# Thirty-eight dummy products on TensorE behind tile 0's scores in a gated cross-attention kernel

## What is computed

```python
x = x + tanh(g_xattn) * xattn(layernorm(x), ctx)
x = x + tanh(g_ffn) * ffn(layernorm(x))
# xattn, 16 heads of 32; with 128 context rows only the image branch has keys
q = rms_norm(xn @ q_w.T + q_b) * norm_q
k = rms_norm(ctx @ k_img_w.T + k_img_b) * norm_k_img
v = ctx @ v_img_w.T + v_img_b
out = softmax(q k^T / sqrt(32)) v  per head, then @ o_w.T + o_b
# ffn, hidden 2048, both weights made ternary in groups of 64
h = relu(xn @ ternary(W_fc).T) ** 2
y = rms_norm(h) @ ternary(W_proj).T
```

## Time and profile before

| | us |
|---|---|
| median of 3 runs | 923.18 |
| the runs | 922.71, 923.18, 924.92 |
| the profiled execution's own time | 922.2 |
| its span (first to last instruction) | 920.4 |
| TensorE busy in the span | 873.2 |
| ScalarE busy | 801.4 |
| VectorE busy | 709.5 |
| mean granted clock of TensorE | 0.985 |

### The profile page before, as it was taken

One profiled execution on the slowest core, in us unless ns is written; L12 is line 12 of the kernel. 1 busy time (PEld: TensorE's weight loads), 2 busy tenths in 40 slices (PEclk: granted clock), 3 DMA queues, 4 the chain that ended last, 5 costly groups with the idle time before them and its releaser, 6 DMA issues.

```text
span 920.4 us, 22304 instructions
## 1 busy us (share of the span) xinstructions
PE 873.2 (95%) x7493; PEld 526.6 (57%) x7589; DVE 709.5 (77%) x1546; ACT 801.4 (87%) x1608; POOL 559.8 (61%) x616
## 2 busy tenths in 40 slices
PE   6687789999999999999999999999999999999998
PEld 3243455556556666555566665556566655666675
DVE  6989999988788787878788787878878787876301
ACT  5988999898998888899998888998988889889674
POOL 2312346777667666667677666666776666756476
PEclk9887999999999999999999999999999999999999
DMA  8849676577657766666577656676767556764401
GB/s 346 213 105 206 139 164 110 104 140 128 126 117 127 136 113 101 123 127 128 118 132 126 120 102 122 122 131 116 134 126 123 120 105 124 129 102 84 81 13 47
DMA packets 319890, 115.78 MB, mean 126 GB/s; under 512 B 305184, under 2 KB 305440, under 8 KB 318240
## 3 DMA queue, kind: packets, MB, share of 16 engines
q1 hardware_dynamic: 319776, 114.34, 63.3%
HBM read 30.67 MB, written 8.39 MB: 42 GB/s over the span
## 4 chain that ended last, share of the span: by engine, by line
PE 79%; ACT 3%; issue 2%; POOL 1%; DVE 1%; POOLq 0%; ACTq 0%; DVEq 0%
PE mix_pair L594 12%; PE up_pair L578 11%; PE up_pair L579 11%; PE mix_pair L593 9%; PE score_pair L533 5%; PE score_pair L532 5%; PE score_pair L531 5%; PE mix_pair L531 3%; PE score_ps L533 3%; PE mix_pair L532 3%; PE mix_pair L533 3%; PE score_ps L532 3%; PE score_ps L531 3%; PE score_pair L662 2%; PE score_pair L594 1%
## 5 line engine op out<-in xcount | busy, mean ns | idle before, releaser
L578 PE MATMUL up_pair<-ft_all,w 128*128 128x256 f16 x960 | 214.4, 272 | 1.9 <-DMA ft_all<-x_rows 0.9
L579 PE MATMUL up_pair<-ft_all,w 128*128 128x256 f16 x960 | 214.4, 272 | 0.0
L2178 POOL TENSOR_TENSOR big<-h_all,big 128x512 f16<-128x512 f32 x128 | 154.0, 1203 | 56.8 <-ACT h_all L1026 38.0
L594 PE MATMUL mix_pair<-w,big 128*128 128x512 bf16 x464 | 175.9, 379 | 7.0 <-issue 4.1
L2188 POOL TENSOR_TENSOR h_all<-h_all,hh_sb 128x512 f32<-128x512 f32 x112 | 142.8, 1275 | 27.9 <-ACT hh_sb L1044 26.4
L593 PE MATMUL mix_pair<-w,big 128*128 128x512 bf16 x383 | 145.2, 379 | 0.3 <-POOL big L2178 0.2
L2133 POOL TENSOR_TENSOR ln_rstd<-ln_in,minus_half 128x1 f32<-128x1 f32 x64 | 45.4, 710 | 112.0 <-issue 90.7
L578 PEld LDWEIGHTS up_pair<-ft_all,w 128*128 128x128 bf16 x960 | 93.7, 98 | 18.0 <-ACT h_all L1017 1.1
L579 PEld LDWEIGHTS up_pair<-ft_all,w 128*128 128x128 bf16 x960 | 93.8, 98 | 15.5
L1086 ACT ACTIVATE score_ps<-score_ps,exp_bias,exp_scale 128x128 f32<-128x128 f32 x256 | 94.9, 443 | 0.0
L1086 ACT ACTIVATE score_pair<-score_pair,exp_bias,exp_scale 128x128 f32<-128x128 f32 x256 | 94.1, 431 | 0.1
(11 more groups left out here) (234 smaller groups left out, 2296.0 us busy)
## 6 DMA issues: line engine op xcount, KB each, us to landing
x_sb<-in_x SPq DMA_DIRECT2D x32, 256.0 KB, 3.5
ctx_sb<-in_ctx_t SPq DMA_DIRECT2D x32, 256.0 KB, 3.6
out<-out_sb SPq DMA_DIRECT2D x31, 256.0 KB, 3.4
big<-in_w_proj_t SPq DMA_DIRECT2D x4, 1024.0 KB, 6.0
big<-in_w_fc_t SPq DMA_DIRECT2D x2, 1024.0 KB, 6.8
pt<-p_rows SPq DMA_TRANSPOSE x128, 3.2
big<-in_wq_t SPq DMA_DIRECT2D x1, 1024.0 KB, 4.9
big<-in_wk_t SPq DMA_DIRECT2D x1, 1024.0 KB, 7.5
```

Of the source, the lines that this page charges most:

```text
L578: nc.tensor.matmul(dst[:, half], w, ft[i][:, c, :], start=(c == 0), stop=False)
L579: last = nc.tensor.matmul(dst[:, half], w, ft[i][:, C + c, :], start=False, stop=(c == C - 1))
L594: last = nc.tensor.matmul(dst[:, cols], ht_lo[i][:, row], w2[:, m, cols], start=False, stop=(m == M - 1))
L2178: nc.gpsimd.tensor_tensor(ht_lo[i][:, rows], h_sb[k % 3][:, :], ht_hi[i][:, rows], ALU.subtract).then_inc(hlo_ready, 1)
```

## The change

One line is added to TensorE's list: 38 dummy products of 384 columns after tile 0's scores and ahead of tile 1's query product.

```diff
             constant_row()
             scores(0)
+            warm(38)
             next_queries(0)
             next_keys(0)
             values(0)
```

## The result

The changed kernel takes 923.87 us (median of 21 runs, 922.11 to 926.06), the kernel before 922.61 us (21 runs beside it, 921.18 to 924.92). The ratio is 1.0016, with a 95% interval of 1.0008 to 1.0023: some 1.3 us slower, clear of noise, and half of the 0.3% that the prediction called the limit of what counts. The prediction said 923.2 us and no change on the path. Its 923.2 rests on a median of three runs of the kernel before; over 21 runs that median is 922.61.

A forecast was written before the change was run, and what follows sets the result against it. The prediction took ACT and DVE to bound the start and TensorE the rest. Dummies, query and key, values and second fall each counted 0, leaving 923.2 us, the median of the runs shown; range 920.9 to 925.4.

The forecast's parts named there:

- The dummies' own cost: TensorE's idle time after tile 0's scores: 38 dummies take 6.2 us, end 0.6 us before it does, cost 0.
- Query and key products: Tile 1's query and key products: each 1.9 us earlier at full clock, but DVE comes later anyway; worth 0 to -0.1.
- The second fall: Clock half from about 49.5 to 56.3 us, slowing tile 1's value product by 2.38 us; kept, 0 to +0.7.
- rival B: Thin work from 44.6 to 50.4 us makes the clock fall more surely or earlier: 923.9 to 925.6 us; chance 0.17.
- The sum: Dummies, query and key, values and second fall each 0, so the profiled execution stays 922.2 and the median 923.2 us.
- A: Clock state at 50 us comes out full, tile 1's value product 2.38 us shorter: at best 920.8 us; chance 0.12.
- C: Dummies run at half clock, ending at 43.8, so DVE gets the key product 2.5 us late: 925.7 us; chance 0.03.
- D: The dummies don't hold the clock, nothing changes on the path: 923.2 us; counted within the forecast's 0.66.
- theory T: From the experiments: a longer thin stretch after the dummies costs time by a second clock fall, earlier or more surely.

The follow-up runs named there:

- e3_thin: The changed kernel with its 38 dummies cut from 384 columns to 2, against the kernel before: 923.97 us, ratio 1.0015.
- e2_again: The changed kernel measured once more without a further edit, against the kernel before: ratio 1.0012.
- e10_shift: The changed kernel with 90 products of 2 columns right behind the 38 dummies, ahead of the query product, against the kernel before: 923.48 us, ratio 1.0001.
- e6_block: The changed kernel with 90 products of 2 columns ahead of tile 0's values, 256 added instructions in all, against the kernel before: 923.30 us, ratio 1.0014.
- e11_block2: The changed kernel with 90 products of 2 columns ahead of tile 0's values, measured a second time, against the kernel before: 923.91 us, ratio 1.0010.
- e1_same: The kernel before, unchanged, measured against itself: 922.34 us against 922.30, ratio 0.9997.
- e7_fill_only: The kernel before with only 12 wide dummies, among tile 0's value blocks and around the context spread, without the 38: ratio 1.0002.
- e5_thin_block: The kernel before with 128 products of 2 columns (256 instructions) in the idle time, against the kernel before: ratio 1.0006.
- e4_fill: The changed kernel with more 384-column dummies, among tile 0's value blocks and around the context spread, against the kernel before: 920.31 us, ratio 0.9979.
- e8_late: The kernel before with 60 wide dummies and 68 of 2 columns ahead of tile 1's query product, against the kernel before: 923.25 us, ratio 1.0010.
- e9_thin64: The kernel before with 64 products of 2 columns (128 instructions) in the idle time, against the kernel before: ratio 1.0009.

## Why the prediction was right, and the term that it lacked

*The dummies' own cost.* Predicted 6.2 us, done by 38.3, cover 0.6 us. Measured 6.35 us and 0.52 us of cover. Right.

*Query and key products.* Predicted 2.59 us each at full clock, worth 0. Measured: query from 38.42 to 41.02; DVE took both without a wait, and PE stood idle 2.23 us for the third block of values, predicted 2.4. Right, and e3_thin shows it from the other side: without the wide columns the time is the same, 923.97 us beside e2_again's 923.64. The runs with 256 added instructions bear it out in part: 1.0006 and 1.0002 without wide dummies, 1.0001 with them in e10_shift, but 1.0014 and 1.0010 in e6_block and e11_block2.

*The second fall.* Kept at its 2.38 us: measured 4.29 for the value product, and ACT's wait 1.87 in place of 2.36. The fall came near 48 us and not at 49.5, and the value product got its full clock back earlier, at 55 and not at 56.3. That looks like rival B, but isn't evidence for it: the kernel before itself had its fall at 47.7 in e1_same and took 4.42 us for the product, and the changed kernel's fall in e2_again came at 50.3, with 3.48 us. The place of this fall differs between executions of one text by some 2 us, as the prediction held possible; its sign for rival B, a fall before 48 us, can't tell the kernels apart.

*"The sum": the step that failed.* The prediction said that no DMA is added or moved. No DMA of the kernel is; but the fetches of TensorE's own program are, and they run on the same engines as the transposes. In the sum this was a term of 0, not named. Measured, it is 0.67 us between tiles 5 and 6, 0.82 between tiles 6 and 7 and 1.49 behind tile 31 in the profile. The three profiles with 76 added instructions all have the last two losses, whether the products are wide or narrow. Of the other eleven rows of the table none has the first of these two, and of the second only e7_fill_only has more than 0.13 us (0.56). That 76 instructions at this place do this, and not the activity or the mere count, is shown by e3_thin and e5_thin_block together.

*The rivals.* A (the clock saved beyond 50 us) did not come with this change but was made real by e4_fill: predicted at best 2.4 us, measured 2.0. C (late dummies) was made real by e8_late: a new wait of 1.84 us where 2.1 was worked out for it; what C costs in the end is not shown, since the clock's gain and a fetch stand in the same profile. D is out: all seven profiles with 38 or 60 wide dummies there have the clock at 1.00 up to 48 us, and all seven without have it fall between 34.1 and 36.6 us. The forecast was right to the size that matters, and partly by luck: it lies 0.7 us from the measured time because the median it started from was 0.6 us high, and the 1.3 us came from something that no rival held.

*What stays open.* The profiles lose 2.3 to 2.8 us in the two steps, the medians only 1.3 to 1.7. Part of it is that the 76-instruction profiles reach tile 6 0.2 to 0.7 us earlier than that of before; the rest is not settled. Nor is it why e6_block and e11_block2 have medians 0.6 and 0.9 us above those of before beside them, while their profiles show spans of 920.0 and 920.4. Those profiles are of the second fastest of twelve executions each. Executions of one text lie 4 us and more apart, and one profile each can't tell how often a packet meets a transpose. Part of this scatter goes with the clock of the start: in the three sets of the kernel before, the executions with a mean granted clock of 0.985 took 921.3, 921.3 and 921.8 us in the mean, those with 0.981 and 0.983 took 922.9 to 923.3. So a share of theory T in e6_block and e11_block2 is not ruled out.

## What to carry to other kernels

Padding work is not free where an engine's program streams in by DMA: count added instructions as a shift of every later fetch, and look whether the waits that are new in the profile stand far from the edit. To separate an operation's work from its mere presence, run it once with the work taken out (2 columns for 384) and once with a whole packet of instructions added. And keep a clock up to the product that somebody waits for: the first fall cost nobody anything, the second cost ACT 2.4 us. Last, profile a text twice before a difference of a microsecond or two in its start is put down to an edit: the kernel before, against itself, showed 1.65 us.

## What the runs showed of the hardware

A transpose with a 16 KB packet of TensorE's instructions in its flight landed 1.1 to 1.8 us later in the changed kernel: 5.1 and 4.5 us against 3.3 and 3.1 at 181 to 185 us, and 4.2 against 3.1 for the transpose of the normed rows at 841 us. Not every such packet costs: in e4_fill and e9_thin64, at 181 and 185 us, the same two transposes landed in 3.8 to 4.2 us and TensorE did not wait. Between tile 7 and tile 31 fourteen profiles keep their distance from each other to 0.02 us: there a lead or a delay of the start is neither won back nor lost.
